# One attention and feed-forward layer on one core: transposed scores divided anew, a pair's order rewritten, batch-end steps moved

## What is computed

```python
xn = layernorm(x)                                  # x: 8 batches x 1024 rows x 512
q, k, v = split(xn @ W_attn + b_attn)              # 16 heads of 32
att = softmax(where(causal, q @ k.T * 32**-0.5, -inf))
y = (att @ v) @ W_proj + b_proj
ffn = fp4_linear(silu(fp4_linear(xn, w_gate)) * fp4_linear(xn, w_up), w_down)
out = x + y + ffn                                  # fp4_linear: both operands rounded to blocks of 16
```

## Time and profile before

| | |
|---|---|
| profiled execution, its own time | 3577.77 us |
| its span, first to last instruction | 3575.8 us |
| mean granted TensorE clock | 0.999 |
| PE busy | 3510.3 us (98%) |
| DVE, ACT, POOL busy | 2688.8, 1217.6, 1103.0 us |
| attention, by the slices of the page | about 23 of 40 slices |

### The profile page before, as it was taken

How to read it: one execution, slowest core, us unless ns; L and a number is a source line. 1 busy time by engine, 2 the same in 40 slices (tenths; PEclk the granted TensorE clock), 3 DMA queues, 4 the chain that set the end, 5 groups by cost and what they waited for, 6 DMA issues and landing times.

```text
span 3575.8 us, 55225 instructions
## 1 busy us (share of the span) xinstructions
PE 3510.3 (98%) x19892; PEld 2607.0 (73%) x19892; DVE 2688.8 (75%) x4872; ACT 1217.6 (34%) x2292; POOL 1103.0 (31%) x552
## 2 busy tenths in 40 slices
PE   8999999999999999999999999999999999999999
PEld 6557567566576575675665688888888888888887
DVE  6786876877877768778777677777777777777776
ACT  2542543534615525435335222222222222222222
POOL 1770952934817709529338100000000000000000
PEclk9999999999999999999999999999999999999999
DMA  6535446346365355363465410110110110110010
GB/s 220 133 100 188 105 146 172 83 154 170 82 197 133 109 180 116 134 183 83 139 189 161 177 32 29 35 35 27 35 35 26 35 35 28 34 35 31 31 35 30
DMA packets 182895, 348.94 MB, mean 98 GB/s; under 512 B 42960, under 2 KB 50640, under 8 KB 181840
## 3 DMA queue, kind: packets, MB, share of 16 engines
q1 hardware_dynamic: 158256, 291.75, 28.4%
q10 hardware_dynamic: 24480, 55.06, 4.3%
HBM read 225.19 MB, written 120.00 MB: 97 GB/s over the span
## 4 chain that ended last, share of the span: by engine, by line
PE 78%; DVE 6%; issue 6%; POOL 3%; DMA 3%; ACT 2%; SPq 1%; ACTq 0%; POOLq 0%; DVEq 0%
PE f_ps L1691 27%; PE f_ps_o L1703 13%; PE ps_dense L1164 12%; PE ps_st L1216 6%; PE ps_s L1189 5%; PE ps_dense L1242 3%; PE ps_y L1242 3%; POOL stage L688 2%; PE ps_dense L1254 2%; PE f_ps L1683 2%; PE ps_dense L1189 1%; POOL stage L686 1%; DVE yt_low L803 1%; PE ps_dense L1330 1%; PE ps_st L1225 1%
## 5 line engine op out<-in xcount | busy, mean ns | idle before, releaser
L1691 PE MATMUL f_ps<-wgu,xqt 128*128 128x512 f32 (+1 forms) x4608 | 990.2, 372 | 1.7 <-DVE xqt L1546 1.4
L1691 PEld LDWEIGHTS f_ps<-wgu,xqt 128*128 128x128 f32 x4608 | 840.4, 188 | 122.7 <-DVE xqt L1546 1.6
L1066 ACT ACTIVATE pt<-ps_st 128x512 f32<-128x512 f32 (+3 forms) x1152 | 543.6, 525 | 448.8 <-PE ps_st L1216 306.8
L761 DVE CUSTOM_DVE_ANT_0 ps_s<-ps_s,row_mask 128x640 f32<-128x640 f32 (+3 forms) x512 | 529.9, 1035 | 126.8 <-PE ps_s L1189 122.6
L1703 PE MATMUL f_ps_o<-wd,hqt 128*128 128x512 f32 x2112 | 512.1, 395 | 0.6 <-DVE hqt L1572 0.6
L1703 PEld LDWEIGHTS f_ps_o<-wd,hqt 128*128 128x128 f32 x2112 | 392.0, 188 | 79.4 <-DVE hqt L1572 0.8
L1164 PE MATMUL ps_dense<-arena,wa 128*128 128x512 f32 x1536 | 378.2, 395 | 0.3 <-DVE stage L818 0.3
L686 POOL TENSOR_TENSOR stage<-pt 128x1792 f32<-128x1792 f32 x41 | 164.9, 4021 | 564.2 <-ACT pt L1066 546.0
L1164 PEld LDWEIGHTS ps_dense<-arena,wa 128*128 128x128 f32 x1536 | 284.8, 188 | 60.9 <-issue 3.8
L688 POOL TENSOR_TENSOR stage<-stage,pt 128x1536 f32<-128x1536 f32 (+2 forms) x107 | 321.4, 3004 | 15.7 <-ACT pt L1066 8.2
L1216 PE MATMUL ps_st<-arena 98*128 98x512 f32 (+3 forms) x768 | 247.4, 390 | 4.7 <-ACT pt L1066 2.2
(11 more groups left out here) (166 smaller groups left out, 5425.1 us busy)
## 6 DMA issues: line engine op xcount, KB each, us to landing
qk_scratch<-stage SPq DMA_DIRECT2D x128, 512.0 KB, 3.0
stack<-qk_scratch SPq DMA_DIRECT2D x192, 256.0 KB
arena<-qk_scratch SPq DMA_DIRECT2D x192, 256.0 KB
xs<-in_L_attn_x SPq DMA_DIRECT2D x64, 256.0 KB, 3.8
acc_scratch<-rob ACTq DMA_DIRECT2D x64, 256.0 KB, 2.0
xt<-in_L_attn_x SPq DMA_DIRECT2D x64, 256.0 KB, 2.6
at<-acc_scratch SPq DMA_DIRECT2D x64, 256.0 KB, 2.7
out<-ot SPq DMA_DIRECT2D x64, 256.0 KB, 2.0
```

What stands on the lines that cost most here:

```text
L761: nc.vector.tensor_tensor_reduce(row, row, row_mask[:, S - keys:S], -1.0, LARGEST, ALU.add, ALU.min, mx[:, h * ST + q:h * ST + q + 1]).the ...
L1066: nc.scalar.activation(exps(kt)[:, heads[0], q - kt * P:q - kt * P + n], ps_st[:, w % ST_RING, 0:n], ACT.Exp, scale=SCALE).then_inc(st_exp, 1)
L1691: last = nc.tensor.matmul(ps[:, SLOT[c], gu, 0:n].rearrange("p (j n) -> p j n", n=P), xqt[:, a, k], wgu[:, b, gu * FC + f // P:gu * FC + ( ...
```

## The change

1. **Parts.** Each key tile's scores are divided from the far end: first 512 (or 384) columns of each head that lie past the diagonal's 256, then a short remainder of both heads together, then the 256 columns from the diagonal on, of both heads in one bank. One mask product serves both heads. A pair has 20 parts in place of 22, 32 score products in place of 24, and 8 mask products in place of 14; the columns are the same.
2. **Order.** `STEPS` and `VECTOR_STEPS` are rewritten. The key tiles' products with v stand in five V visits (P3 P4; P5 P6 P7; DEN P0; P1; P2) where there were six. `MAX` stands at the start of key tile 5 instead of the end of key tile 3. `Y0` and `Y1` move apart and ahead.
3. **Sums.** GpSimd adds (8, 7, 8, 7, 7, 6, 5, 3) key tiles for the eight pairs instead of (8, 8, 8, 8, 8, 8, 5, 3); TensorE does the rest with ones.
4. **Batch end.** Before the last pair's `invert`, VectorE runs one `low_of_y` instead of two. The fourth `transpose_x` and its `low_of_x` go behind the first finished output tile. The first unit's split comes one step earlier; the second unit's transpose and split come behind all eight output tiles.

```diff
-    PAIRED = 6
...
+    def parts_of(kt):
+        first, parts = kt * P + DIAG, []
+        while S - first >= QC - P:
+            n = min(QC, S - first)
+            parts += [(range(h, h + 1), first, n) for h in range(2)]
+            first += n
+        if first < S:
+            parts.append((range(2), first, S - first))
+        return [*parts, (range(2), kt * P, min(DIAG, S - kt * P))]
...
+    SUMMED = (8, 7, 8, 7, 7, 6, 5, 3)
...
-             "S0 S1 P2 S2 M2 S3 M3 MAX",
+             "T T S0 S1 P1 T T S2 M2",
...
+             "MAX T S0 S1 M1",
+             "S0 T M0",
+             "S0 M0 T"]
...
-    VECTOR_STEPS = "R R R R R R R Y0 Y1 DEN R R R R R R INV MAX R R R"
+    VECTOR_STEPS = "R R R R R Y0 R R Y1 R DEN R R R R R INV MAX R R R"
...
-                            for g in range(SPLIT - 1):
-                                low_of_y(g)
+                            low_of_y(0)
                         if p:
                             invert(p - 1)
                         if p == PAIRS - 1 and not final:
+                            for g in range(1, SPLIT - 1):
+                                low_of_y(g)
...
-                for t in range(XR):
+                for t in range(XR - 1):
                     low_of_x(b + 1, t)
...
                 add(k)
+                if k == 0 and not final:
+                    low_of_x(b + 1, XR - 1)
...
-                if k == 5:
+                if k == 4:
                     low_of_unit(one)
-                if k == 7:
-                    low_of_unit(two)
+            low_of_unit(two)
...
-                if k == 4:
+                if k == 3:
                     high_of_unit(one)
                 if k == 6:
-                    high_of_unit(two)
                     store_unit(one)
+            high_of_unit(two)
             store_unit(two)
...
-            if not final:
-                transpose_x(b + 1, XR - 1)
...
+                if k == 0 and not final:
+                    transpose_x(b + 1, XR - 1)
                 if k == 4:
                     transpose_unit(one)
-                if k == 6:
-                    transpose_unit(two)
+            transpose_unit(two)
```

More of the change, by code:

```diff
@@ L63, in attention @@
     KM = KS + 2
-    PAIRED = 6
-    PARTS = [[(range(h, h + 1), max(c * QC, kt * P), (c + 1) * QC - max(c * QC, kt * P))
-              for c in reversed(range(NQ)) if (c + 1) * QC > kt * P for h in range(2)] for kt in range(PAIRED)]
-    PARTS += [[(range(2), kt * P, (ST - kt) * P)] for kt in range(PAIRED, ST)]
+    DIAG = 2 * P
+    def parts_of(kt):
[7 more added lines that the diff above has]
+        return [*parts, (range(2), kt * P, min(DIAG, S - kt * P))]
+    PARTS = [parts_of(kt) for kt in range(ST)]
     NPARTS = sum(len(parts) for parts in PARTS)
@@ L83, in attention @@
     TAIL = 2 * P * sum(ST - k for k in range(RINGED, ST))
+    SUMMED = (8, 7, 8, 7, 7, 6, 5, 3)
     def summed(p):
-        return ST if p < PAIRS - 2 else RINGED if p < PAIRS - 1 else 3
+        return SUMMED[p]
     SUM_ORDER = [*range(1, ST)]
@@ L97, in attention @@
     TILE = [(h, q) for h in range(2) for t in range(ST // 2) for q in (ST // 2 + t, ST // 2 - 1 - t)]
-    STEPS = ["T T S0 S1 T P3 T S2 S3 T M2 M3",
[7 rows of a table removed]
-    VECTOR_STEPS = "R R R R R R R Y0 Y1 DEN R R R R R R INV MAX R R R"
+    STEPS = ["S0 S1 S2 T S3 T P3 P4 T T M3",
+             "S0 S1 T P5 P6 P7 T S2 S3 M3 T",
+             "S0 S1 T S2 DEN P0 M2",
+             "T T S0 S1 P1 T T S2 M2",
+             "S0 S1 T M1 P2",
+             "MAX T S0 S1 M1",
+             "S0 T M0",
+             "S0 M0 T"]
+    VECTOR_STEPS = "R R R R R Y0 R R Y1 R DEN R R R R R INV MAX R R R"
     FLAT = " ".join(STEPS).split()
@@ L1068, in body @@
                         else:
-                            nc.scalar.activation(exps(kt), ps_st[:, w % ST_RING, 0:2 * n].rearrange("p (h n) -> p h n", h=2),
+                            nc.scalar.activation(exps(kt)[:, :, q - kt * P:q - kt * P + n],
+                                                 ps_st[:, w % ST_RING, 0:2 * n].rearrange("p (h n) -> p h n", h=2),
                                                  ACT.Exp, scale=SCALE).then_inc(st_exp, 1)
@@ L1216, in transposed_scores @@
                     last = nc.tensor.matmul(ps_st[:, w % ST_RING, j * n:(j + 1) * n], stack(p)[0:KM, 2 + h, kt * P:(kt + 1) * P],
-                                            stack(p)[0:KM, h, q:q + n], start=j == 0, stop=not diagonal)
+                                            stack(p)[0:KM, h, q:q + n], start=j == 0, stop=not diagonal and j == len(heads) - 1)
                 if not diagonal:
@@ L1254, in denominators @@
                         last = nc.tensor.matmul(by_tile(den_bank(p)[y_rows(h, s)]), ones[:, :], by_tile(sums(p, h, final))[:, s::2],
-                                                start=True, stop=summed(p) == ST)
+                                                start=True, stop=summed(p) >= ST - 1 + s)
                 for kt in range(summed(p), ST):
```

## The result

| | before | changed |
|---|---|---|
| median of the runs | 3577.04 us | 3638.28 us (3628.82 to 3647.21) |
| profiled execution: its time, span, mean granted clock | 3577.8, 3575.8, 0.999 | 3636.7, 3634.7, 0.984 |

The ratio is 1.0171, with a 95% interval of 1.0144 to 1.0198. The change costs 61 us where 28 were forecast, and the median lies 2 us above the wider range of 3553 to 3636.

A forecast was written before the change was run, and what follows sets the result against it. PE was taken as the bound in middle pairs. 72 + 10 + 5 - 9 - 36 + 5 - 19 = +28 us on the profiled 3577.8 gave 3606, median 3605; own range 3588 to 3630, with rivals 3553 to 3636.

The forecast's parts named there:

- the wider range: Whole kernel: 3553 to 3636 us, the forecast's range once several of the rivals are taken in.
- late landings: Maxima's DMAs landing later than the 1.8 us median, lateness no longer hidden: between 0 and +20 us, +5 taken.
- the trip of the maxima: `MAX` to `S0`: trip stays 3.44 us, only 2.3 us of products stand behind `MAX`, PE waits about 1.1 us.
- the forecast's own: Whole kernel: 3588 to 3630 us, the range with the unknown terms of the forecast alone.
- The two inner waits: Between `S0` and `MAX`: 0.3 us for the fourth part's weights, 0.5 us for VectorE's copy of the denominators.
- The sum's +1.8 us: `S0` to `MAX` in pairs 2 to 6: 1.8 us longer each, 40 times, +72 us.
- PE's list: PE's products without waits: 16.6 us a pair instead of 17.84, 14.3 of them between `S0` and `MAX`.
- The 0.37 us of the visit: PE's saving a pair from one V visit fewer, its cost beyond streaming.
- Here PE itself is the bound: Middle pairs of the kernel before: PE goes from product to product, 17.84 us a pair, trip of the maxima hidden.
- The batch's end: `S0` of pair 7 to next batch: 48.07 us become about 45.6 through earlier inversion and fewer PE stops; -19 us.
- Rival 2: Inside the pair: VectorE's and ScalarE's waits do not arise, the copy ends half a microsecond earlier; 3556 us, chance 0.17.
- Rival 5: Maxima's DMAs run into later pairs' loads, one in three late, and batch end gives nothing; 3637 us, chance 0.15.

## Why the prediction was right or wrong

The sum by stretches, `S0` to `S0` over all batches, with half of the low stretches taken out as the clock's part (an estimate; the forecast's terms are put to the stretch in which they fall):

| stretch | forecast | measured |
|---|---|---|
| pairs 2 to 6 | 72 - 32 x 0.76 - 4 = +44 | +27 |
| pairs 0 and 1 | 15 - 16 x 0.76 - 5 = -2 | -4 |
| pair 7 to the next batch, and the last end | -19 | -18 |
| late landings | +5 | in the rows above |
| clock | none | half of 109.2: +55 |

- **The step that failed is the trip of the maxima.** "PE waits about 1.1 us at every `S0`" was right (0.93 us), but the step priced that wait as its own length. Its second price, the stretch at half clock that follows in about half of the pairs, is some 55 us, and no rival named it. Without it the profiled execution would stand at 3636.7 - 54.6 = 3582 us, 24 below the 3606 forecast for it: inside the wider range, below the forecast's own of 3588 to 3630. That the time came out only 2 us above the wider range is luck: a missing 55 us and an excess of 24 partly cancel.
- **The two inner waits** came, nearly where they were forecast, though the profile counts little of either as idle time of PE. Pair 4 of the third batch again, the weight load of the fourth part and VectorE's copy:

```profile
684.81 0.30 PEld L1228 LDWEIGHTS ps_st<-stack 98*128 98x128 f32 x2 [0.39 <-ACT pt L1077]
693.17 0.69 DVE L788 COPY rob<-ps_dense 128x512 f32<-128x512 f32 x1
```

The fourth part starts 1.27 us behind `S0` (1.25 forecast), its weights held by ScalarE. The copy ends at 693.86, 10.32 us behind `S0` (10.5 forecast), and the tile that needs its bank starts at 693.91. In all 17 of pairs 2 to 6 that kept their clock up to `MAX` this tile starts 0.05 to 0.06 us behind the copy's end, which lies at 10.31 to 10.49 us. Behind it 4.72 us lead to `MAX` (4.7 forecast). So 15.09 us is the forecast path, a little shorter. The sum's +1.8 us (15.33) was too much by the prediction's own figures: 14.3 + 0.3 + 0.5 is 15.1, and 10.5 + 4.7 is 15.2; over 40 pairs that is 5 to 9 us of the 17 by which the first row was too high.
- **PE's list** of 16.6 us is not confirmed and not refuted: the measured 15.09 + 2.52 = 17.6 us hold both inner waits, and no run is without them. A mask uncovered costs at most 0.05 us, not 0.12; six masks are at most 0.3 us, not 0.72. The 0.37 us of the visit did not show in any run. Of the spacings read from the earlier trace rows one holds a wait for VectorE that the profile shows as busy: the tile at 666.51 starts 0.05 us behind the read of a maximum that ends at 666.46. Those from which the mask and the visit were priced do not; why the mask came out too dear stays open. "Here PE itself is the bound" was half right: VectorE paced the old order too.
- **The batch's end** was right, in size and by its reason.
- **Rivals.** Rival 2's condition, a copy that ends half a microsecond earlier than 10.5, did not come true. Rival 5's 3637 is near the result for reasons that did not act: landings were not late in one pair of three, and the batch's end gave what was forecast.

## What to carry to other kernels

Price an uncovered wait of PE not by its length alone: look at the granted clock in the stretch behind it. Here a wait of 0.93 us cost 1.7 us on average in the changed kernel, and waits up to 1.28 us cost no more than their own length in the middle pairs of the kernel before. So a wait's price from one kernel must not be carried to another unmeasured. Before taking a spacing on a "100% busy" PE as the price of a product, look whether the instruction starts a few hundredths of a microsecond behind another engine's release; if so, what is saved there is given back at once. And an edit that shortens the critical engine's list by moving the hand-over must be judged by what is left behind that hand-over.

## What was not expected of the hardware

- Half-clock stretches of 3.41 us after waits of about 1 us, on a PE that is busy 97% of the span; the same wait 18.5 us later often leaves the clock at 1.00, and in the kernel before waits of 1.1 to 1.3 us always did in pairs 1 to 6.
- Two small DMAs issued together on two queues land 0.3 us apart (2.76 and 3.07 us behind `MAX`), though the first of two on one queue lands at 2.77.
- Twelve added products, or eight added masks, in 17.85 us cost 0.03 and 0.08 us in the order in which VectorE paces PE.
